# Redrawn job places within an iteration, and epsilon as the bias of ScalarE's root, in a macaron block on one core

## What is computed

```python
x = x + 0.5 * ffn(layernorm(x))      # ffn(z) = z W^T + b + (z V_r) C^T, folded into one 256 x 256 matrix
x = x + attention(layernorm(x))      # 16 heads of 16; causal; weights polymax(s), no row sum
x = x + 0.5 * ffn(layernorm(x))
# polymax(s) = (s*s + 1)/1000 for s > 0, (1 - s/100)/1000 for -100 <= s <= 0
# layernorm(x) = (x - mean) / sqrt(var + 1e-5)
```

## Time and profile before

| | us |
|---|---|
| runs | 1924.37 median, 1923.38 to 1930.8 (3 runs) |
| profiled execution, its own time | 1931.65 |
| its span | 1929.9 |
| PE busy in the span | 1665.2 (86%) |
| DVE, ACT, POOL busy | 1361.7, 1363.2, 1326.5 (69 to 71%) |

### The profile page before, as it was taken

How to read it: one execution, slowest core, us unless ns; L and a number is a source line. 1 busy time by engine, 2 the same in 40 slices (tenths; PEclk the granted TensorE clock), 3 DMA queues, 4 the chain that set the end, 5 groups by cost and what they waited for, 6 DMA issues and landing times.

```text
span 1929.9 us, 66983 instructions
## 1 busy us (share of the span) xinstructions
PE 1665.2 (86%) x27158; PEld 814.6 (42%) x27158; DVE 1361.7 (71%) x3313; ACT 1363.2 (71%) x2178; POOL 1326.5 (69%) x1419
## 2 busy tenths in 40 slices
PE   4677789898989989898998989898898999898785
PEld 2343334343444435353443535344444444443342
DVE  1465677777777867778786777878676778787672
ACT  1244568787888777777877877777787788888561
POOL 3344558787778868777676877867677767686552
PEclk8888889999999999999999999999999999999897
DMA  2344433241424233341523334241324222323111
GB/s 75 124 128 129 114 106 108 83 110 49 133 67 136 85 103 95 99 132 50 159 66 111 87 106 128 71 135 57 117 86 130 86 72 80 82 73 78 49 37 59
DMA packets 155191, 183.14 MB, mean 95 GB/s; under 512 B 22012, under 2 KB 129660, under 8 KB 152836
## 3 DMA queue, kind: packets, MB, share of 16 engines
q1 hardware_dynamic: 154884, 178.82, 31.6%
HBM read 102.43 MB, written 76.30 MB: 93 GB/s over the span
## 4 chain that ended last, share of the span: by engine, by line
PE 54%; DVE 15%; ACT 12%; issue 8%; POOL 8%; DMA 2%; SPq 0%; ACTq 0%; POOLq 0%; DVEq 0%
PE y_ps L991 20%; PE score L991 16%; PE bank L991 14%; DVE rp L926 9%; ACT rp L831 4%; ACT rp L851 3%; PE bank L1017 3%; POOL rp L735 2%; POOL z L697 2%; ACT rp L847 2%; DVE lin L932 2%; DMA part_scratch<-parts 1%; POOL rp L710 1%; POOL parts L465 1%; DMA x1c<-x_scratch 1%
## 5 line engine op out<-in xcount | busy, mean ns | idle before, releaser
L926 DVE TENSOR_SCALAR rp<-score 128x512 f32<-128x512 f32 (+2 forms) x1728 | 944.1, 573 | 276.0 <-PE score L991 271.3
L991 PE MATMUL score<-qs,ks 96*32 96x512 bf16 (+3 forms) x10240 | 742.7, 354 | 137.8 <-DVE rp L926 74.6
L735 POOL TENSOR_TENSOR rp<-rp 128x1024 f32<-128x1024 f32 (+1 forms) x416 | 756.3, 1830 | 125.1 <-DVE rp L926 114.1
L831 ACT ACTIVATE rp<-score 128x512 f32<-128x512 f32 (+1 forms) x832 | 458.4, 592 | 267.8 <-PE score L991 266.2
L991 PE MATMUL y_ps<-rp,vt 128*16 128x512 f32 (+3 forms) x5120 | 597.8, 537 | 24.3 <-ACT rp L851 13.3
L991 PEld LDWEIGHTS score<-qs,ks 96*32 96x32 bf16 x10240 | 294.4, 96 | 547.9 <-DVE rp L926 266.8
L847 ACT ACTIVATE rp<-rp,rise 128x1024 f32<-128x1024 f32 (+1 forms) x416 | 462.6, 1144 | 1.7 <-POOL rp L710 1.7
L710 POOL TENSOR_SCALAR_AFFINE_SELECT rp<-rp 128x256 f32<-128x256 f32 (+1 forms) x384 | 185.2, 484 | 317.2 <-DVE rp L926 161.5
L851 ACT ACTIVATE rp<-rp 128x1024 f32<-128x1024 f32 (+2 forms) x224 | 291.1, 1305 | 131.4 <-DVE rp L926 66.0
L932 DVE SCALAR_TENSOR_TENSOR lin<-score,slope_mask 128x128 f32<-128x128 f32 x768 | 214.4, 279 | 0.0
L991 PEld LDWEIGHTS y_ps<-rp,vt 128*16 128x16 f32 x5120 | 134.4, 97 | 111.5 <-ACT rp L851 25.7
(11 more groups left out here) (78 smaller groups left out, 1360.0 us busy)
## 6 DMA issues: line engine op xcount, KB each, us to landing
part_scratch<-parts SPq DMA_DIRECT2D x16, 1536.0 KB, 7.5
qs<-part_scratch SPq DMA_DIRECT2D x384, 64.0 KB
ks<-part_scratch SPq DMA_DIRECT2D x384, 64.0 KB, 2.4
state_scratch<-st_new SPq DMA_DIRECT2D x16, 528.0 KB
st<-state_scratch SPq DMA_DIRECT2D x64, 132.0 KB
x_sb<-in_L_attn_x_dram SPq DMA_DIRECT2D x16, 512.0 KB, 4.4
x_scratch<-x SPq DMA_DIRECT2D x16, 512.0 KB, 5.4
qT_scratch<-qkT SPq DMA_DIRECT2D x16, 512.0 KB, 3.8
```

Of the source, the lines that this page charges most:

```text
L735: pool.tensor_tensor(half, half, half, ALU.mult).then_inc(squared["pool"], 1)
L831: nc.scalar.activation(rp[T % RP_BUFS][:, 2 + v, off:CH], score[H % S_BUFS][:, v, off:CH], ACT.Relu).then_inc(raised["act"], 1)
L926: nc.vector.tensor_scalar(rp[T % RP_BUFS][:, 2 * u + v, off:CH], score[H % S_BUFS][:, v, off:CH], 0.0, RISE, ALU.max, ALU.add).then_inc(ra ...
L991: return nc.tensor.matmul(*args, start=start, stop=stop, skip_group_check=True)
```

## The change

Three tables get other numbers. In the sum with epsilon, the separate DVE instruction goes: ACT's root reads the variance where the aggregation left it and adds epsilon as its bias. DVE's wait for the normalised rows of the chunk before moves from the reciprocal to the aggregation, which now overwrites what ACT reads. One memset on POOL and renumbered counts for the constants come with it.

```diff
-A_FULL = {"z1T": (32, 34), "ffn": (38, 42), "z2T": (61, 63), "ln1": 8, "ln2": 45}
-B_FULL = {"qT": (0, 6), "k": (8, 12), "v": (16, 20), "kT": (46, 52), "state": (48, 54, 56, 58)}
-C_FULL = {"proj": (24, 28), "ln3": 32, "z3T": (65, 67), "out": (71, 75)}
+A_FULL = {"z1T": (36, 36), "ffn": (38, 43), "z2T": (61, 65), "ln1": 12, "ln2": 50}
+B_FULL = {"qT": (1, 6), "k": (8, 12), "v": (16, 20), "kT": (41, 47), "state": (53, 59, 61, 63)}
+C_FULL = {"proj": (24, 26), "ln3": 32, "z3T": (57, 68), "out": (70, 75)}
...
+        eps = sb("eps", [P, 1])
...
+            pool.memset(eps[:], EPS).then_inc(const_ready, 1)
...
-                        act.wait_ge(var_done[k], chunk + 1)
-                        nc.scalar.activation(sd[k][:], var[k][:], ACT.Sqrt).then_inc(sd_done[k], 1)
+                        act.wait_ge(aggr_done[k], (chunk + 1) * NB)
+                        nc.scalar.activation(sd[k][:], mv[k][:, :, 1], ACT.Sqrt, bias=eps[:]).then_inc(sd_done[k], 1)
...
                 dve.wait_ge(stats_done[k], (chunk + 1) * NB)
+                if chunk > 0:
+
+                    dve.wait_ge(z_ready[k], chunk)
                 for i in range(NB):
                     nc.vector.bn_aggr(mv[k][:, i, :], bnst[k][:, i, :]).then_inc(aggr_done[k], 1)
-                dve.wait_ge(aggr_done[k], (chunk + 1) * NB)
-                nc.vector.tensor_scalar(var[k][:], mv[k][:, :, 1], EPS, None, ALU.add).then_inc(var_done[k], 1)
...
                 dve.wait_ge(sd_done[k], chunk + 1)
-                if chunk > 0:
-
-                    dve.wait_ge(z_ready[k], chunk)
```

More of the change, by code:

```diff
@@ L348, in build @@
         mv = {k: sb(f"mv_{k}", [P, NB, 2]) for k in LNS}
-        var = {k: sb(f"var_{k}", [P, NB]) for k in LNS}
         sd = {k: sb(f"sd_{k}", [P, NB]) for k in LNS}
@@ L384, in build @@
         aggr_done = {k: sem(f"aggr_{k}") for k in LNS}
-        var_done = {k: sem(f"var_done_{k}") for k in LNS}
         sd_done = {k: sem(f"sd_done_{k}") for k in LNS}
@@ L417, in build @@
         waits_met = {e.engine: sem(f"waits_met_{i}") for i, e in enumerate((nc.gpsimd, nc.sync))}
-        CONSTS = 15
+        CONSTS = 16
         K_LOADS, Q_LOADS = len(PAIRS) + 1, len(PAIRS) + 2
@@ L664, in _ @@
             pool.memset(rise[:], RISE).then_inc(const_ready, 1)
-            pool.wait_ge(const_ready, 8)
+            pool.memset(eps[:], EPS).then_inc(const_ready, 1)
+            pool.wait_ge(const_ready, 9)
             pool.affine_select(out=slope_mask[:], in_=slope_mask[:], compare_op=ALU.is_ge, fill=0.0, base=0,
@@ L672, in _ @@
                                pattern=[[0, QUADS], [-HD, QH], [0, HD]], channel_multiplier=1).then_inc(const_ready, 1)
-            pool.wait_ge(const_ready, 11)
+            pool.wait_ge(const_ready, 12)
             pool.affine_select(out=smask[:], in_=smask[:], compare_op=ALU.is_ge, fill=0.0, base=HD,
@@ L677, in _ @@
             for odd in range(2):
-                pool.wait_ge(const_ready, 12 + odd)
+                pool.wait_ge(const_ready, 13 + odd)
                 rows = by_parity[:, :, odd, :]
@@ L682, in _ @@
             pool.wait_ge(w_loaded, 16 * 6)
-            pool.wait_ge(const_ready, 14)
+            pool.wait_ge(const_ready, 15)
             pool.tensor_scalar(bias_half[:], bias_half[:], 0.5, 0.0, ALU.mult, ALU.add).then_inc(const_ready, 1)
```

## The result

| | before | after |
|---|---|---|
| median of 8 runs each, us | 1926.65 (1923.28 to 1930.8) | 1942.16 (1934.99 to 1944.94) |
| ratio, 95% interval | | 1.0077 [1.0061, 1.0094] |
| span of the profiled execution, us | 1929.9 | 1943.2 |

The change costs 15.5 us. That is inside the range of 1893 to 1952 and above the forecast's own range of 1914 to 1937. "No change" was called likeliest, at 0.40; "slower by over 0.5%", at 0.32, is what happened. The interval of the ratio lies clear of 1.

What follows compares the result with a forecast made beforehand. PE was taken as the bound, with 11.0 us idle per iteration to win. Terms +6.3, -2.0, -3.3, -1.0 and +3 (clock) sum to +3.0: 1934.7 us profiled, 1927.4 median; own range 1914 to 1937, wider range 1893 to 1952.

Steps and rivals of the forecast that it cites:

- Part 1: Slots 46 to 61: states and kT leave DVE's raises; gain of at most 5.5 us per iteration.
- Part 2: Both z1T jobs in slot 36: the ffn piece starts 1.9 us later, bounds 0.5 and 3.0.
- Part 3: Slots 49 to 62: z2T waits 5 to 6 us for POOL's queue; net of parts 1 to 3, slot 62 0.9 later.
- The rule of the Trainium skill on the shift: Shifts of ln2 (slot 58) and ln1 (slot 20): DVE and GpSimd exclude each other, blocking DVE up to 4 us.
- Part 4: z3T's second piece to 68, out to 70: out waits 2.2 us; net +0.3 us, between -0.9 and +2.2.
- the other two moves: Values' wait for tile 33's square (0.6) and out's first emptying off a raise (0.75): 1.35 us returned.
- the rest shifts: Remainder at z3T and out, given without a size of its own, in the net of +0.3 us.
- Rival 2: Slower, 1951: out's wait stays whole (+17) and ln1's shift blocks DVE (+7); chance 0.32.
- Rival 2's other half: ln1's shift blocks DVE among whole tiles: +0.7 us in ten iterations, +7.
- Part 5: Remaining edits, together -0.3 us per full iteration; dropping the sum with epsilon about 1 us in all, in prologue and end.
- The clock: Falls to 1.2 GHz after the idle stretch in four more iterations, 1.6 us each, half hidden: +3 us.
- Iterations 1 to 3: No ln3 bias rows on POOL, chain starts earlier, ffn waits 0.9 less: -0.65 us each, -2.0.

Runs made afterwards that it cites:

- e7: Only the four state jobs moved to 53, 59, 61 and 63, against the kernel before's tables with the new root: 1886.89 us, ratio 0.98.
- e1: The new root alone (epsilon as bias, wait moved to the aggregation) in the tables of the kernel before: 1911.75 us, ratio 0.9935.
- e3: The changed kernel with z1T back at slots 32 and 34: 1930.63 us, ratio 1.0038 to the kernel before.
- e5: The changed kernel with z3T's second piece at slot 66 instead of 68: 1915.91 us, ratio 0.9958 to the kernel before.
- e8: The changed kernel with z1T (32, 34), ffn (38, 43), ln1 8, ln2 46, proj (24, 26), z3T (57, 66), out (70, 75): 1835.95 us.
- e9: e8 with the old sum with epsilon on DVE: 1838.66 us, ratio 0.9571 to the kernel before.
- e4: The changed kernel with five extra 128x512 matmuls ahead of PE's wait for z2T in iterations 1 to 10: 1925.41 us, ratio 1.0002 to the kernel before.
- e10: The kernel before with the same five extra matmuls ahead of z2T in iterations 1 to 10: 1970.0 us, ratio 1.0252.
- e2: The changed kernel with z2T four slots later, at (65, 67): 1894.58 us, ratio 0.9862 to the kernel before.

## Why the prediction was right and wrong

- **Part 1, right in kind, half in size.** PE's waits for DVE's raises fell from 74.6 to 16.0 us. Alone the move of the states gives 2.3 to 3 us an iteration (e7 against e1), and part of what it wins in slots 46 to 61 (3.6 us in iteration 6) goes again behind slot 62 (1.0), where POOL's squares become late; 5.5 was the stated upper bound.
- **Part 2, right.** Said: the ffn piece starts 1.9 us later. It starts 10.9 us after slot 32 (882.23 - 871.3) for 8.9 before, 2.0 later, and e3 gives 1.9 back.
- **Part 3, right, and the best step of the working.** Said: a queue of 19.6 us, a wait of 5 to 6, slot 62 0.9 later. Measured: 19.5, 5.53, and 1.1. (The 27.0 us beside which it sets POOL's 23.1 are slots 46 to 61, not 49 to 61; nothing hangs on it.) The shift of ln2, for which up to 4 us was weighed, took 1.55 us in its new slot and was not what set the wait, since POOL had no idle time ahead of the rows of z. Of the signs that were to show the forecast right all came: the wait and the full POOL queue, 1.63 us in slot 38 and 2.30 in slot 70, and in iteration 6 no wait for DVE's raises between slots 49 and 60. The start of the queue came out as said as well: 25.7 us after slot 32 was said (894.9 - 869.2), 25.6 measured (896.94 - 871.3).
- **The rule of the Trainium skill on the shift** ("SBUF — State Buffer", "Who interferes with whom") is borne out in kind: an operation of 128 x 4 lasted 1.55 us in the changed kernel and 3.31 in e1, both beside POOL's squares. Each ended within 0.03 us of the end of the squares beside it: one square in the changed kernel, two without a gap in e1. At slot 20 ln1's shift stood beside no square but a mask, ended with it, and took 0.50 us. DVE's and POOL's rows, of the changed kernel and then of e1:

```profile
907.18 1.55 DVE L883 SCALAR_TENSOR_TENSOR shift_ln<-mv_ln,rstd_ln 128x4 f32<-128x4 f32 x1
906.82 1.89 POOL L735 TENSOR_TENSOR rp<-rp 128x1024 f32<-128x1024 f32 x1
```

```profile
889.21 3.31 DVE L883 SCALAR_TENSOR_TENSOR shift_ln<-mv_ln,rstd_ln 128x4 f32<-128x4 f32 x1
888.75 3.74 POOL L735 TENSOR_TENSOR rp<-rp 128x1024 f32<-128x1024 f32 x2
```

- **Part 4, its waits right, its net wrong.** Said: out waits 2.2 us, the other two moves return 1.35, net +0.3. The wait is 2.30, and the moves return what was said (1.4, e5). That leaves 0.85 by the prediction's own numbers and 1.0 measured; the +0.3 needs another 0.55 from "the rest shifts", for which it gives no row. The clock took another 1.3, for which part 4 has no term. e5 prices this place at 26.3 us in all. Rival 2 named the place and gave it 17 us of these 26.3, but for another reason: it had the moves return nothing. Its sign, over 4 us of idle time in slots 70 to 79, did not show: 3.47.
- **Rival 2's other half, wrong.** Slots 0 to 31, where ln1's shift was to block DVE, became 1.1 us faster, and the shift took 0.50 us there.
- **Part 5, the epsilon, not settled.** Said: about 1 us, as "DVE isn't late in the places that now set the time". In the tables of before it is worth 14 us (e1). There DVE is late, as part 1 itself says; that this is why is likely, but not shown, since e1 also moves a wait and lets ACT start earlier. In e8's tables it can't be told from zero (e9). In the changed tables, of which the prediction speaks, it wasn't measured, so whether this term is wrong stays open. What the prediction did not see is that the root has a worth of its own elsewhere: with it in both kernels, the tables cost 30 us.
- **The clock, the step that failed.** Said: +3 us, four more iterations of 1.6, half hidden. The traces have 64.8 us more at 1.2 GHz between 290 and 1700 us (85.3 for 20.5). Filling the wait of slot 61 alone gives 16.7 us back (e4), and the clock's share in slots 70 to 79 goes away with e5. With some 17 us for it instead of 3, the forecast of 1927.4 would have been 1941; measured are 1942.2. That it comes so near is partly luck, since other terms missed in both directions. The page "TensorE: Matmul & The Clock Gate", section "What's actually happening", in the Trainium skill says that for modelling the penalty of the ramp is under 1% of a typical kernel's span. It speaks of the ramp at a kernel's start, which no run here prices; the falls in the middle are a further 0.9% of this kernel by e4, about as much as the whole change (0.8%).
- **Iterations 1 to 3, wrong sign.** Said -2.0, measured +2.9. They have the same wait for z (5.53 us in iteration 2; the clock there fell from 0.99 to 0.97), while I had counted on POOL's chain to start earlier.

## What to carry to other kernels

When a move turns several short waits of the bounding engine into one long one, count the long one dearer than its length: first add up the queue ahead of it on the engine that makes its operand, then add what the matmuls behind it lose at the lower clock. Add an in-order queue up by hand before moving a job; with durations from the trace, that came within 0.2 us here. And where a change holds several edits, price each in both surroundings, since the same edit was worth 14 us in one table and in another 3 to 5, which can't be told from nothing.

## What the chip did that I had not expected

Giving PE more to do made the kernel faster: 50 extra matmuls and 16.7 us less, where the same 50 cost 47.5 us in the kernel without that wait (e4, e10). The clock of the 7 us behind a wait of 5.5 us was 0.62, and behind one of 2.3 us it still fell (0.90 over slots 70 to 79), as it did around one of 1.84 us in e2 (0.87 over slots 62 to 69). The kernel before, with single waits of up to 1.5 us, kept 1.00 in all of iteration 6. Waits of 0.97 us (e4) and 1.14 us (e8) did not bring it down in iteration 6 either, nor did the 1.63 us in slot 38 of the changed kernel. But the length of one wait doesn't decide it: in iteration 7 of the kernel before, with the same waits of 0.69 and 1.54 us, the clock was 0.50 from 1023.0 to 1026.2 us.
